# Last destination tile of the first attention: its high and low part in one set of weights, its chain on 160 columns

## The chip, the cores and the metric

The kernel runs on one core of one Trainium2 chip. The metric is the device time of one execution in microseconds. Before the change three runs gave 2427.32, 2428.82 and 2431.33 us; the median is 2428.82.

## The reference, cut to what matters

Four graph layers run one behind the other on 2708 nodes with 512 features. The change is in layer 0, whose attention is a softmax over the neighbours and a second softmax of the negated scores.

```python
def _L0_gnn_ref(inp, adj, W, a, wtrans):          # layer 0
    h = inp @ W
    e = leaky_relu(h @ a[:512] + (h @ a[512:]).T, 0.2)
    mask = adj > 0
    attention = softmax(where(mask, e, -1e12), axis=1)
    negative_attention = -softmax(where(mask, -e, -1e12), axis=1)
    h_prime_double = concatenate([attention @ inp, negative_attention @ inp], axis=1)
    return elu(h_prime_double @ wtrans)

def reference(x, adj, ...):                        # x: 2708 x 512, adj: 2708 x 2708
    h = maximum(layernorm(x), 0); x = x + _L0_gnn_ref(h, adj, ...)
    h = maximum(layernorm(x), 0); x = x + _L1_gnn_ref(h, adj, ...)   # 8 heads
    h = maximum(layernorm(x), 0); x = x + _L2_gnn_ref(h, adj, ...)   # weighted midpoint
    h = maximum(layernorm(x), 0); x = x + _L3_gnn_ref(h, adj, ...)   # dense scores
    return x
```

## The kernel before, in words

The 2708 nodes are padded to T = 22 tiles of 128. The last tile has 20 real rows (LAST = 20). The function `attention0` computes layer 0's attention with destinations in 11 blocks (IB = 11) of two tiles each, so that a block is 256 columns wide (BW). For each block `ib` and each source tile `j` there is a unit `m = 22 ib + j`; the last block is units 220 to 241, called units 0 to 21 of the last block below.

A unit goes through a chain over three engines. ScalarE makes the relu of the scores (`relu`), VectorE adds two rows for the two softmaxes (`scores`), ScalarE takes two exponentials (`exp`), VectorE multiplies with the mask (`mask`), ScalarE rounds to 16 bits (`high`, into `p_hi`), and VectorE takes what the rounding lost (`low`, into `p_lo`). `p_hi` and `p_lo` have five buffers (RP = 5); before it writes a buffer the chain waits for `p_used`, which TensorE counts up when it has done a unit. TensorE takes these as weights, 128 source rows by 128 destination columns, and multiplies with `z`, the features already multiplied with the layer's weights, also in a high and a low part. Each product has three terms: high by `z_hi`, high by `z_lo`, low by `z_hi`. Each term is a pair of matmuls with the same weights: 448 columns into `acc` and the other 64 (65 with the column of ones that gives the softmax's sum) into `side`. So `products` issues, for each of the two destination tiles (`q` is 0 or 1) and each of the two softmaxes (`s`), three pairs: 12 pairs a unit. The last source tile, `j` = 21, has only 20 rows, and there all terms are packed into one set of rows, so one matmul does for three.

TensorE's order is written out: in each block the first two units of tile 0, then the first two of tile 1, and after that both tiles of each unit. The engines run in order and wait for counters. When a block's sums are there, `denominator` makes the reciprocals on VectorE, `minus` and `minus_side` scale the negative half on ScalarE, `evacuate` and `evacuate_side` subtract on VectorE, `isolated` puts the mean in for nodes without neighbours, and `elu`, `plus` and `finish` add the result to x. For blocks 0 to 9 these steps are woven into the next block's chain. For block 10 they stand alone behind the last unit, and the next stage (`prep1`) starts after them.

SyncE's queue loads the mask and the rows of scores a block ahead, loads x, and stores x (`store_x`). Beside the chain the last block converts the mask to 8 bits (`convert`) and prepares the first rows for the next stage (`first_rows`, and a square root on ScalarE at `j` = 9).

Of the kernel before, what the change touches and what calls it, by code (L numbers as in the profile page):

```python
# [11 lines left out]
ALU = mybir.AluOpType  # L12
# [5 lines left out]
P = 128  # L18
# [583 lines left out]
def attention0(nc, dram, keep):  # L602
    with ExitStack() as stack:
# [17 lines left out]
        den = kit.sb("den", [2, 2])  # L621
        acc = kit.ps("acc", [3, 2, D])
# [13 lines left out]
            "blank_made v_packed z_packed ones_made os_made ys_made")  # L636

# [5 lines left out]
        with nc.Block() as block:  # L643
# [79 lines left out]
            def _(act):  # L723
                def relu(m):
# [7 lines left out]
                    act.activation(r[:, m % RR, :], u_row[:, ib % 2, :], ACT.Relu, bias=keep["v08"][:, j:j + 1],  # L732
                                   scale=0.8).then_inc(r_made, 1)

                def exp(m):
                    j = m % T
                    act.wait_ge(sc_made, m + 1)
                    if m >= RE:
                        act.wait_ge(pm_made, m - RE + 1)
                    act.activation(e[:, m % RE, 0], sc[:, m % RS, 0], ACT.Exp, bias=keep["v02"][:, j:j + 1])  # L740
                    act.activation(e[:, m % RE, 1], sc[:, m % RS, 1], ACT.Exp, bias=negv[:, j:j + 1], scale=-1.0).then_inc(e_made, 1)  # L741

                def high(m):
# [3 lines left out]
                    act.activation(p_hi[:, m % RP], pm[:, m % RM], ACT.Copy).then_inc(hi_made, 1)  # L747
# [24 lines left out]
                def minus(ib, q):  # L772
# [6 lines left out]
                    act.activation(o[:, q, 0:CA], acc[:, n % 3, 1, 0:CA], ACT.Identity, scale=den[:, q, 1:2], bias=one[:, 0:1]).then_inc(o_made, 1)  # L779

                def minus_side(ib):

                    for q in range(2):
                        act.activation(o[:, q, CA:D], side[:, ib % 2, q, 1, 0:DH], ACT.Identity, scale=den[:, q, 1:2], bias=one[:, 0:1]).then_inc(os_made, 1)
# [11 lines left out]
                for m in range(UNITS):  # L796
# [27 lines left out]
            def _(dve):  # L824
                def scores(m):
# [6 lines left out]
                    dve.tensor_tensor(sc[:, m % RS], r[:, m % RR, :].unsqueeze(1).broadcast_to([P, 2, BW]), g_row[:, ib % 2],  # L832
                                      ALU.add).then_inc(sc_made, 1)

                def mask(m):
# [8 lines left out]
                    dve.scalar_tensor_tensor(pm[:, m % RM], e[:, m % RE], TOP,  # L844
                                             at32[:, half, part, :].unsqueeze(1).broadcast_to([P, 2, BW]), ALU.min, ALU.mult).then_inc(pm_made, 1)

                def low(m):
# [2287 lines left out]
```

## Time and profile before

| | |
|---|---|
| median of three runs | 2428.82 us |
| the profiled execution: its own time | 2428.78 us |
| its span, from the first to the last instruction | 2426.9 us |
| TensorE busy | 2252.2 us, 93% of the span |
| VectorE busy | 1715.3 us, 71% |
| ScalarE busy | 1569.4 us, 65% |
| granted clock of TensorE, mean | 0.973 of full speed |
| matmuls of the first attention, first to last start | 176.2 to 807.5 us |

A row of the trace in order of time gives the start and the duration in microseconds, the engine (PE is TensorE, PEld its weight loads, DVE is VectorE, ACT ScalarE, SPq SyncE's queue), the line, what is written and read, the shape, and in brackets how long the engine had been idle and what ended that. For a matmul the shape is first rows*columns of the weights, then rows x columns of the moved operand. The recorded durations of matmuls overlap, since they are pipelined; what one costs in a row of many is the distance from start to start. Shares of the whole span are averages over stages; for a change in one stage the rows of that stage count.

### The profile page before, as it was taken

To read this page: it belongs to the slowest core of one execution; us is meant where nothing else is said; L and a number is where in the kernel's file an instruction comes from. 1 tells how busy PE (TensorE), PEld (TensorE's weight loads), DVE (VectorE), ACT (ScalarE), POOL (GpSimd) and SP (SyncE) were. 2 spreads that over 40 slices of the span, in tenths; PEclk is the share of its full clock that TensorE was granted. 3 is DMA by queue.
4 is the path that set the end of the run, shared out by engine and by line. 5 is a ranking of instruction groups with operands and counts; after the bars stand their busy time and mean duration, and the time that the engine had idled before them with its cause. 6 is when DMAs were issued, how large, how long until landed. Compare 5 with 4: busy or idle time off the path is not lost. (4 is left out here: it accounts for less than half of the span.)

```text
span 2426.9 us, 69291 instructions
## 1 busy us (share of the span) xinstructions
PE 2252.2 (93%) x29240; PEld 1469.5 (61%) x29240; DVE 1715.3 (71%) x3033; ACT 1569.4 (65%) x2622; POOL 35.3 (1%) x44
## 2 busy tenths in 40 slices
PE   7979999999999787999999867799989899999999
PEld 4535555555555447999999863355467545555554
DVE  5857888888887678999999965832467344556784
ACT  3448888888888468999999957521245444444452
POOL 1210000000000000000000000000000000000000
PEclk9989999999999898999999989999989999999999
DMA  4022222232222552121211125011111234334441
GB/s 176 9 80 66 84 84 84 85 100 95 84 83 86 185 191 64 34 52 52 51 52 52 60 64 177 13 37 41 32 70 49 79 102 125 106 103 130 114 129 36
DMA packets 224468, 201.05 MB, mean 83 GB/s; under 512 B 148972, under 2 KB 181906, under 8 KB 219964
## 3 DMA queue, kind: packets, MB, share of 16 engines
q1 hardware_dynamic: 222604, 189.11, 25.7%
q10 hardware_dynamic: 1584, 7.93, 1.0%
q8 instruction: 209, 3.42, 0.6%
q14 instruction: 71, 0.58, 0.1%
HBM read 145.37 MB, written 51.46 MB: 81 GB/s over the span
## 5 line engine op out<-in xcount | busy, mean ns | idle before, releaser
L1464 ACT ACTIVATE m_above<-keep_u,m_nvs 128x1408 fp8e5<-128x1408 f32 x318 | 435.5, 1453 | 0.0
L968 PE MATMUL m_acc<-keep_z_hi,m_p_hi 128*128 128x448 f16 x968 | 337.9, 353 | 19.8 <-DVE m_p_lo L852 16.9
L968 PE MATMUL m_acc<-keep_z_hi,m_p_lo 128*128 128x448 f16 x924 | 326.0, 353 | 0.0
L968 PE MATMUL m_acc<-keep_z_lo,m_p_hi 128*128 128x448 f16 x924 | 324.6, 351 | 0.0
L1805 PE MATMUL m_acc<-right_x_all,m_b 128*128 128x64 f16 x3872 | 242.6, 195 | 18.3 <-DVE m_b L1521 15.0
L1805 PE MATMUL m_acc<-right_x_all,m_c 128*128 128x64 f16 x3872 | 238.7, 194 | 14.4 <-DVE m_c L1529 11.2
L1805 PEld LDWEIGHTS m_acc<-right_x_all,m_b 128*128 128x128 fp8e5 x3872 | 233.7, 100 | 18.6 <-DVE m_b L1521 15.8
L1809 PE MATMUL m_acc<-right_x_all,m_b 128*128 128x64 f16 x3696 | 241.4, 195 | 1.8 <-issue 1.8
L1809 PE MATMUL m_acc<-right_x_all,m_c 128*128 128x64 f16 x3696 | 237.5, 194 | 4.0 <-issue 3.8
L1805 PEld LDWEIGHTS m_acc<-right_x_all,m_c 128*128 128x128 fp8e5 x3872 | 228.6, 99 | 16.5 <-DVE m_c L1529 12.9
L1809 PEld LDWEIGHTS m_acc<-right_x_all,m_b 128*128 128x128 fp8e5 x3696 | 230.0, 99 | 3.5 <-issue 3.3
L1809 PEld LDWEIGHTS m_acc<-right_x_all,m_c 128*128 128x128 fp8e5 x3696 | 226.4, 98 | 4.4 <-issue 4.4
L972 PE MATMUL m_side<-keep_z_hi,m_p_hi 128*128 128x65 f16 x968 | 183.6, 193 | 0.0
L972 PE MATMUL m_side<-keep_z_hi,m_p_lo 128*128 128x65 f16 x924 | 180.2, 195 | 0.0
L747 ACT ACTIVATE m_p_hi<-m_pm 128x512 f16<-128x512 f32 x242 | 151.3, 625 | 41.4 <-PE m_side L972 36.6
L844 DVE SCALAR_TENSOR_TENSOR m_pm<-m_e,m_at 128x512 f32<-128x512 f32 x242 | 166.6, 689 | 15.5 <-ACT m_e L741 3.7
L972 PE MATMUL m_side<-keep_z_lo,m_p_hi 128*128 128x64 f16 x924 | 177.2, 192 | 0.0
L2739 PE MATMUL m_acc<-keep_s_hi,m_wT_hi 128*128 128x512 f16 (+1 forms) x462 | 175.1, 379 | 0.0
L2741 PE MATMUL m_acc<-keep_s_hi,m_wT_lo 128*128 128x512 f16 (+1 forms) x462 | 175.1, 379 | 0.0
L2740 PE MATMUL m_acc<-keep_s_lo,m_wT_hi 128*128 128x512 f16 (+1 forms) x462 | 175.1, 379 | 0.0
L832 DVE TENSOR_TENSOR m_sc<-m_r,m_ug_row 128x512 f32<-128x512 f32 x242 | 166.1, 687 | 12.1 <-ACT m_r L732 10.6
L2968 ACT ACTIVATE m_lw<-m_sc 128x512 f32<-128x512 f32 (+3 forms) x70 | 32.1, 468 | 218.9 <-DVE m_mx L2785 188.8
(406 smaller groups left out, 5757.1 us busy)
## 6 DMA issues: line engine op xcount, KB each, us to landing
m_at<-adjT SPq DMA_DIRECT2D x11, 1408.0 KB, 7.0
m_at<-adjT SPq DMA_DIRECT2D x11, 1280.0 KB
keep_u<-rows SPq DMA_DIRECT2D x16, 704.0 KB, 4.1
low<-m_lw SPq DMA_DIRECT2D x32, 256.0 KB, 5.1
at<-edge_at SPq DMA_DIRECT2D x22, 352.0 KB, 3.2
keep_at<-at ACTq DMA_DIRECT2D x11, 704.0 KB, 6.5
keep_at_first<-at SPq DMA_DIRECT2D x22, 352.0 KB, 3.4
p_x_all<-x SPq DMA_DIRECT2D x4, 1536.0 KB, 10.3
```

The lines of the kernel that those rows point to most:

```text
L747: act.activation(p_hi[:, m % RP], pm[:, m % RM], ACT.Copy).then_inc(hi_made, 1)
L832: dve.tensor_tensor(sc[:, m % RS], r[:, m % RR, :].unsqueeze(1).broadcast_to([P, 2, BW]), g_row[:, ib % 2], ALU.add).then_inc(sc_made, 1)
L844: dve.scalar_tensor_tensor(pm[:, m % RM], e[:, m % RE], TOP, at32[:, half, part, :].unsqueeze(1).broadcast_to([P, 2, BW]), ALU.min, ALU.mu ...
L968: return pe.matmul(acc[:, n % 3, s, of], part(m, q, s, low), z[:, m % T, s, of], start=first, stop=last, skip_group_check=True)
L972: return pe.matmul(side[:, m // T % 2, q, s, 0:columns], part(m, q, s, low), z[:, m % T, s, CA:CA + columns], start=first, stop=last, skip ...
L1464: last = act.activation(above[:, q % RA, j - j0], u[:, g % RU], ACT.Relu, bias=nvs[:, g // NB, j:j + 1], scale=STEEP, saturate=False)
L1805: last = pe.matmul(to, mask, of[:, j0 + j, n, 0], start=(n == 0 and ch == 0 and j == 0 and t % 4 == 0), stop=(j0 + j == T - 1), skip_group ...
L1809: last = pe.matmul(to, mask, of[:, j0 + j, n, 1], start=False, stop=False, skip_group_check=True)
L2739: pe.matmul(acc[0:r, b, :], wT_hi[:, b, k, 0:r], s_hi[:, k, :], start=(k == 0), stop=False)
L2740: pe.matmul(acc[0:r, b, :], wT_hi[:, b, k, 0:r], s_lo[:, k, :], start=False, stop=False)
L2741: last = pe.matmul(acc[0:r, b, :], wT_lo[:, b, k, 0:r], s_hi[:, k, :], start=False, stop=False)
L2968: last = act.activation(lw[:, slot, 0:hi - lo], sc[:, q % SB, lo - n0:hi - n0], ACT.Copy)
```

## The change

In the last block the second destination tile has only 20 real columns. The change treats it as E = 32 columns. The chain of the last block works on 128 + 32 = 160 columns of each softmax in place of 256 (`width`). The low part of the 32 columns is written into `p_hi` directly behind the high part, so that one set of weights of 64 columns holds both. `products` calls `last_tile` for this tile: with `z_hi` it uses these 64 columns, and writes 64 rows of `acc` and `side` (high part in rows 0 to 31, low part in rows 32 to 63); with `z_lo` it uses the 32 columns of the high part. That makes two pairs for each softmax in place of three. Behind the last unit `move_low` copies rows 32 to 63 on ScalarE, and `add_low` and `add_wide` add them to rows 0 to 31 on VectorE. The flags of the rows from 32 on are filled with 1.0 by two memsets. `denominator` now waits for the first sum, and `minus` of the last tile for both.

```diff
+        E = 32
+        low_part, low_sum = kit.sb("low_part", [2, D]), kit.sb("low_sum", [2])
+        width = lambda m: BW if m < UNITS - T else P + E
+        rows_of = lambda ib, q: slice(0, E if (ib, q) == (IB - 1, 1) else P)
...
-                    act.activation(p_hi[:, m % RP], pm[:, m % RM], ACT.Copy).then_inc(hi_made, 1)
+                    act.activation(p_hi[:, m % RP, :, 0:width(m)], pm[:, m % RM, :, 0:width(m)], ACT.Copy).then_inc(hi_made, 1)
...
+                def move_low():
+
+                    act.wait_ge(acc_made, 2 * IB)
+                    act.activation(low_part[0:E, :, CA:D + 0], side[E:2 * E, (IB - 1) % 2, 1, :, 0:DH], ACT.Copy)
+                    act.activation(low_sum[0:E, :], side[E:2 * E, (IB - 1) % 2, 1, :, DH], ACT.Copy).then_inc(low_moved, 1)
+                    act.activation(low_part[0:E, :, 0:CA], acc[E:2 * E, (2 * IB - 1) % 3, :, 0:CA], ACT.Copy).then_inc(low_moved, 1)
...
+                move_low()
                 minus(IB - 1, 0)
                 minus_side(IB - 1)
                 minus(IB - 1, 1)
...
-                    if m % T < T - 1:
+                    if m % T == T - 1:
+                        low = p_hi[COPIES[2]:P, m % RP, :, 0:width(m)]
+                        dve.tensor_tensor(low, pm[COPIES[2]:P, m % RM, :, 0:width(m)], low, ALU.subtract).then_inc(lo_made, 1)
+                    elif m < UNITS - T:
                         dve.tensor_tensor(p_lo[:, m % RP], pm[:, m % RM], p_hi[:, m % RP], ALU.subtract).then_inc(lo_made, 1)
                     else:
-                        low = p_hi[COPIES[2]:P, m % RP]
-                        dve.tensor_tensor(low, pm[COPIES[2]:P, m % RM], low, ALU.subtract).then_inc(lo_made, 1)
+                        for to, of in ((p_lo[:, m % RP, :, 0:P], slice(0, P)), (p_hi[:, m % RP, :, P + E:P + 2 * E], slice(P, P + E))):
+                            last = dve.tensor_tensor(to, pm[:, m % RM, :, of], p_hi[:, m % RP, :, of], ALU.subtract)
+                        last.then_inc(lo_made, 1)
...
+                def add_low():
+                    dve.wait_ge(low_moved, 1)
+                    last = side[0:E, (IB - 1) % 2, 1]
+                    dve.tensor_tensor(last[:, :, 0:DH], last[:, :, 0:DH], low_part[0:E, :, CA:D], ALU.add)
+                    dve.tensor_tensor(last[:, :, DH], last[:, :, DH], low_sum[0:E, :], ALU.add).then_inc(low_added, 1)
+
+                def add_wide():
+                    dve.wait_ge(low_moved, 2)
+                    last = acc[0:E, (2 * IB - 1) % 3, :, 0:CA]
+                    dve.tensor_tensor(last, last, low_part[0:E, :, 0:CA], ALU.add).then_inc(low_added, 1)
...
+                add_low()
+                dve.wait_ge(low_added, 1)
                 denominator(IB - 1)
+                add_wide()
                 evacuate(IB - 1, 0)
+                dve.wait_ge(rden_made, IB)
+                for rows in (slice(E, 2 * E), slice(2 * E, P)):
+                    last = dve.memset(iso[rows, T - 1:T], 1.0)
+                last.then_inc(low_iso, 1)
+                dve.wait_ge(low_iso, 1)
                 evacuate_side(IB - 1)
                 evacuate(IB - 1, 1)
...
+                def last_tile(m, s, low, z, first):
+
+                    n, end = 2 * IB - 1, P + (2 * E if low else E)
+                    weights = p_hi[:, m % RP, s, P:end]
+                    to, columns = slice(0, end - P), DH + (z is z_hi)
+                    pe.matmul(acc[to, n % 3, s, 0:CA], weights, z[:, m % T, s, 0:CA], start=first, stop=False, skip_group_check=True)
+                    return pe.matmul(side[to, m // T % 2, 1, s, 0:columns], weights, z[:, m % T, s, CA:CA + columns],
+                                     start=False, stop=False, skip_group_check=True)
...
+                    if j < T - 1 and n == 2 * IB - 1:
+                        for s in range(2):
+                            for low, z in ((1, z_hi), (0, z_lo)):
+                                last = last_tile(m, s, low, z, j == 0 and z is z_hi)
+                        last.then_inc(p_used, 1)
+                        return
```

On TensorE, in a unit in the middle of the last block, the second destination tile stood in these rows before, for one of the two softmaxes (the name before the arrow is written, the first number is the number of weight columns, the second the columns moved):

```order
L968 MATMUL m_acc<-keep_z_hi,m_p_hi 128x448
L972 MATMUL m_side<-keep_z_hi,m_p_hi 128x65
L968 MATMUL m_acc<-keep_z_lo,m_p_hi 128x448
L972 MATMUL m_side<-keep_z_lo,m_p_hi 128x64
L968 MATMUL m_acc<-keep_z_hi,m_p_lo 128x448
L972 MATMUL m_side<-keep_z_hi,m_p_lo 128x65
```

With the change the same place, from the last matmul of the first tile to the second softmax of the last tile, reads:

```order
L1030 MATMUL m_side<-keep_z_hi,m_p_lo 128x65
L1015 MATMUL m_acc<-keep_z_hi,m_p_hi 64x448
L1016 MATMUL m_side<-keep_z_hi,m_p_hi 64x65
L1015 MATMUL m_acc<-keep_z_lo,m_p_hi 32x448
L1016 MATMUL m_side<-keep_z_lo,m_p_hi 32x64
L1015 MATMUL m_acc<-keep_z_hi,m_p_hi 64x448
```

Three pairs became two, and the number of weight columns goes from 128 to 64, to 32 and back to 64; behind the second softmax it goes from 32 back to 128.

On VectorE the end of the last block, from the last low part to the last add into x, was:

```order
L855 TENSOR_TENSOR m_p_hi<-m_pm,m_p_hi 64x512
L865 TENSOR_SCALAR keep_iso<-m_side 128x2
L867 SCALAR_TENSOR_TENSOR m_den<-keep_iso,m_side 128x4
L870 RECIPROCAL m_den<-m_den 128x4
L879 SCALAR_TENSOR_TENSOR m_y<-m_acc,m_den,m_o 128x448
L884 SCALAR_TENSOR_TENSOR m_y<-m_side,m_den,m_o 128x64 x2
L879 SCALAR_TENSOR_TENSOR m_y<-m_acc,m_den,m_o 128x448
L889 SCALAR_TENSOR_TENSOR m_y<-keep_cd,keep_iso,m_y 128x512 x2
```

With the change it is:

```order
L872 TENSOR_TENSOR m_p_hi<-m_pm,m_p_hi 64x2x160
L914 TENSOR_TENSOR m_side<-m_side,m_low_part 32x2x64
L915 TENSOR_TENSOR m_side<-m_side,m_low_sum 32x2
L888 TENSOR_SCALAR keep_iso<-m_side 128x2
L890 SCALAR_TENSOR_TENSOR m_den<-keep_iso,m_side 128x4
L893 RECIPROCAL m_den<-m_den 128x4
L920 TENSOR_TENSOR m_acc<-m_acc,m_low_part 32x2x448
L903 SCALAR_TENSOR_TENSOR m_y<-m_acc,m_den,m_o 128x448
L995 MEMSET keep_iso 32x1
L995 MEMSET keep_iso 64x1
L909 SCALAR_TENSOR_TENSOR m_y<-m_side,m_den,m_o 128x64
L909 SCALAR_TENSOR_TENSOR m_y<-m_side,m_den,m_o 32x64
```

Three adds and two memsets came in, two of the adds ahead of the reciprocal. On ScalarE the three copies of `move_low` stand ahead of `minus` in the same way.

## Rows read from the trace of the kernel before

**Rows 1.** Busy time by stretch: last block, then last attention's end; clock behind engines.

```profile
752.50:806.80 54.30, 54.23 (x492) 31.51 (x493) 42.00 (x72) 44.41 (x102) 0.00 (x0) 1.00 0.18 54
...
2408.65:2422.20 13.55, 13.55 (x69) 5.79 (x66) 0.83 (x4) 0.00 (x0) 0.00 (x0) 1.00 0.05 19
```

**Rows 2.** Waits of TensorE from 748 to 812: us, times, longest.

```profile
PE m_acc L968 <- PE m_acc L968: 0.3, 1, 0.3
PE m_acc L968 <- DVE m_p_lo L852: 0.3, 1, 0.3
```

**Rows 3.** TensorE in order of time, last block: start, duration.

```profile
750.79 0.35 PE L968 MATMUL m_acc<-keep_z_hi,m_p_hi 128*128 128x448 f16 x1 [0.30 <-PE m_acc L968]
...
752.57 0.36 PE L968 MATMUL m_acc<-keep_z_hi,m_p_hi 128*128 128x448 f16 x1 [0.29 <-DVE m_p_lo L852]
...
806.83 0.35 PE L968 MATMUL m_acc<-keep_z_hi,m_p_hi 128*128 128x448 f16 x1
...
807.34 0.54 PE L968 MATMUL m_acc<-keep_z_hi,m_p_hi 128*128 128x448 f16 x2
```

**Rows 4.** Order of time in the last attention: matmuls, then weight loads.

```profile
2321.77 0.38 PE L2737 MATMUL m_acc<-keep_s_hi,m_wT_hi 128*128 128x512 f16 x1
2321.98 0.38 PE L2680 MATMUL m_sc<-keep_e_hi 128*128 128x512 f16 x1
...
2391.32 0.38 PE L2737 MATMUL m_acc<-keep_s_hi,m_wT_hi 128*128 128x512 f16 x1
2391.63 0.18 PE L2680 MATMUL m_sc<-keep_e_hi 128*20 128x20 f16 x1
...
2391.91 0.17 PE L2680 MATMUL m_sc<-keep_e_hi,keep_e_lo 128*20 128x20 f16 x1
2392.01 0.28 PE L2695 MATMUL m_tw<-keep_ident,m_w_hi 128*128 128x128 f16 x2
...
2321.77 0.10 PEld L2680 LDWEIGHTS m_sc<-keep_e_hi 128*128 128x128 f16 x1
...
2391.62 0.09 PEld L2680 LDWEIGHTS m_sc<-keep_e_hi 128*20 128x20 f16 x1 [0.42 <-issue]
```

**Rows 5.** TensorE in order of time at the end of the last attention.

```profile
2408.65 0.38 PE L2739 MATMUL m_acc<-keep_s_hi,m_wT_hi 128*20 128x512 f16 x1
...
2422.24 0.38 PE L2737 MATMUL m_acc<-keep_s_hi,m_wT_hi 128*20 128x512 f16 x1
```

**Rows 6.** VectorE and ScalarE in order of time, last block.

```profile
750.63 0.68 DVE L832 TENSOR_TENSOR m_sc<-m_r,m_ug_row 128x512 f32<-128x512 f32 x1
751.22 0.69 DVE L844 SCALAR_TENSOR_TENSOR m_pm<-m_e,m_at 128x512 f32<-128x512 f32 x1
751.82 0.69 DVE L852 TENSOR_TENSOR m_p_lo<-m_pm,m_p_hi 128x512 f16<-128x512 f32 x1
...
750.75 0.73 ACT L779 ACTIVATE m_o<-m_acc,m_one,m_den 128x448 f32<-128x448 f32 x1 [5.41 <-DVE m_den L870]
...
790.72 0.63 ACT L747 ACTIVATE m_p_hi<-m_pm 128x512 f16<-128x512 f32 x1 [0.54 <-DVE m_pm L844]
```

**Rows 7.** Order of time at the end of the last block and behind it.

```profile
801.20 0.38 SPq L671 DMA_DIRECT2D m_x<-x  x1
...
807.59 0.16 DVE L865 TENSOR_SCALAR keep_iso<-m_side 128x2 f32<-128x2 f32 x1 [7.23 <-PE m_side L972]
...
808.19 0.72 ACT L779 ACTIVATE m_o<-m_acc,m_one,m_den 128x448 f32<-128x448 f32 x1 [8.55 <-DVE m_den L870]
808.82 0.69 ACT L784 ACTIVATE m_o<-m_side,m_one,m_den 128x64 f32<-128x64 f32 x2
809.13 0.68 DVE L879 SCALAR_TENSOR_TENSOR m_y<-m_acc,m_den,m_o 128x448 f32<-128x448 f32 x1 [0.97 <-ACT m_o L779]
...
812.44 1.23 DVE L894 SCALAR_TENSOR_TENSOR m_x<-m_y,m_x 128x1024 f32<-128x1024 f32 x1
...
814.95 0.36 SPq L675 DMA_DIRECT2D x<-m_x  x1
```

More of the change, by code:

```diff
@@ L731, in relu @@
                         act.wait_ge(sc_made, m - RR + 1)
-                    act.activation(r[:, m % RR, :], u_row[:, ib % 2, :], ACT.Relu, bias=keep["v08"][:, j:j + 1],
+                    act.activation(r[:, m % RR, 0:width(m)], u_row[:, ib % 2, 0:width(m)], ACT.Relu, bias=keep["v08"][:, j:j + 1],
                                    scale=0.8).then_inc(r_made, 1)
@@ L778, in minus @@
                         act.wait_ge(acc_made, n + 1)
[L779 removed]
+                    if n == 2 * IB - 1:
+                        act.wait_ge(low_added, 2)
+                    of = rows_of(ib, q)
+                    act.activation(o[of, q, 0:CA], acc[of, n % 3, 1, 0:CA], ACT.Identity, scale=den[of, q, 1:2], bias=one[of, 0:1]).then_inc(o_made, 1)
                 def minus_side(ib):
                     for q in range(2):
[L784 removed]
+                        of = rows_of(ib, q)
+                        act.activation(o[of, q, CA:D], side[of, ib % 2, q, 1, 0:DH], ACT.Identity, scale=den[of, q, 1:2], bias=one[of, 0:1]).then_inc(os_made, 1)
+                def move_low():
[3 more added lines that the diff above has]
+                    act.activation(low_part[0:E, :, 0:CA], acc[E:2 * E, (2 * IB - 1) % 3, :, 0:CA], ACT.Copy).then_inc(low_moved, 1)
                 def elu(ib):
@@ L831, in scores @@
                         dve.wait_ge(e_made, m - RS + 1)
-                    dve.tensor_tensor(sc[:, m % RS], r[:, m % RR, :].unsqueeze(1).broadcast_to([P, 2, BW]), g_row[:, ib % 2],
+                    w = width(m)
+                    dve.tensor_tensor(sc[:, m % RS, :, 0:w], r[:, m % RR, 0:w].unsqueeze(1).broadcast_to([P, 2, w]), g_row[:, ib % 2, :, 0:w],
                                       ALU.add).then_inc(sc_made, 1)
@@ L843, in mask @@
                         dve.wait_ge(lo_made, m - RM + 1)
-                    dve.scalar_tensor_tensor(pm[:, m % RM], e[:, m % RE], TOP,
-                                             at32[:, half, part, :].unsqueeze(1).broadcast_to([P, 2, BW]), ALU.min, ALU.mult).then_inc(pm_made, 1)
+                    w = width(m)
+                    dve.scalar_tensor_tensor(pm[:, m % RM, :, 0:w], e[:, m % RE, :, 0:w], TOP,
+                                             at32[:, half, part, 0:w].unsqueeze(1).broadcast_to([P, 2, w]), ALU.min, ALU.mult).then_inc(pm_made, 1)
                 def low(m):
@@ L964, in part @@
                     return (p_hi, p_lo)[low][:, m % RP, s, q * P:(q + 1) * P]
+                def last_tile(m, s, low, z, first):
[5 more added lines that the diff above has]
+                                     start=False, stop=False, skip_group_check=True)
                 def wide(m, n, q, s, low, z, first, last):
                     of = slice(0, CA)
+                    if n == 2 * IB - 1:
+                        return pe.matmul(acc[0:E, n % 3, s, of], p_hi[:, m % RP, s, P:P + E], z[:, m % T, s, of], start=first, stop=last, skip_group_check=True)
                     return pe.matmul(acc[:, n % 3, s, of], part(m, q, s, low), z[:, m % T, s, of], start=first, stop=last, skip_group_check=True)
@@ L971, in narrow @@
                     columns = DH + (z is z_hi)
+                    if m == UNITS - 1 and q == 1:
+                        return pe.matmul(side[0:E, m // T % 2, 1, s, 0:columns], p_hi[:, m % RP, s, P:P + E], z[:, m % T, s, CA:CA + columns],
+                                         start=first, stop=last, skip_group_check=True)
                     return pe.matmul(side[:, m // T % 2, q, s, 0:columns], part(m, q, s, low), z[:, m % T, s, CA:CA + columns],
```

11 lines of the change are left out of this document (7 added, 4 removed).

## The prediction

> **What bounds the kernel now.** I read the busy time by stretch first, then the waits of TensorE, then its instructions in order of time, then the same for the other engines in the last block and behind it. In the last block of the first attention TensorE is busy 54.23 of 54.30 us at the full clock (2.4 GHz), VectorE 42.00 and ScalarE 44.41 [rows 1]. In the whole block it is seen waiting twice, 0.3 us each time [rows 2]. So TensorE bounds this block. A pair of matmuls (448 columns, then 64 or 65) is the unit of cost: from 752.57 to 806.83 there are 246 such pairs (12 in each of 19 units, 18 left over from the first two), 54.26 us, that is 0.2206 us a pair with no stall in between [rows 3].
>
> Behind the block stands a chain in which nothing overlaps: sums, reciprocal, ScalarE's and VectorE's halves of the last tile, the final adds, the store at 814.95 [rows 7], and the next stage starts after it. What is added there is paid in full.
>
> **What the change removes.** In each of units 0 to 20 of the last block the last destination tile took six pairs and now takes four: 2 x 21 = 42 pairs, 42 x 0.2206 = 9.3 us. The moved columns stay 448 and 64 or 65, and the trace shows that weights of few columns do not make a matmul shorter: in the last attention, with 20-column weights, the 512-column matmuls start every 0.216 us (63 steps from 2408.65 to 2422.24), as with 128 columns [rows 4, 5]. So the gain is pairs alone. Nor does the clock fall with narrow weights: 1.00 granted in that stretch [rows 1].
>
> **The stall at the block's start.** VectorE there does scores, mask and low part one behind the other, 0.68 or 0.69 us each, from 750.63 to 752.51 [rows 6], and TensorE, whose six pairs from 750.79 end at about 752.11, starts the next at 752.57 [rows 3]. With 320 elements in place of 512, each of the first two shrinks by about 0.2 us (0.69 for 512, 1.23 for 1024 [rows 6, 7], so 0.54 per 512), the split third by some 0.1. Low parts are then there near 752.05: the stall of 0.46 goes, I take 0.4. Bounds: 0 and 0.5.
>
> **What the change adds on TensorE.** Here is the term that decides. The order of instructions shows that the weights change their number of columns all the time: 128, 64, 32, 64, 32, 128. That is five changes in each unit; units 0 and 1 lie together and have nine. With 19 units of five and three changes in unit 21, that is 9 + 95 + 3 = 107 changes. Before there are none in this block. The trace has few such changes, but it has them. In the last attention the step from a 512-column matmul with 128-column weights to the next with the same kind is 0.21 (2321.77 to 2321.98). Where the next has 20-column weights the step is 0.31 (2391.32 to 2391.63), and on the way back, after a 20-column matmul of which its like start 0.025 apart (eleven steps from 2391.63 to 2391.91), it is 0.10 [rows 4]. The rows of weight loads show the same: normally a load starts with the matmul before it, 2321.77; here it starts at 2391.62, only 0.01 before its own matmul, after 0.42 us of idle time marked "issue" [rows 4]. So both steps are the streaming time plus about 0.095 us: 512 columns take 0.213, 20 take 0.008. All changes of the new order come behind a 64- or 65-column matmul, which streams 0.027 and whose usual step is 0.03; the step becomes 0.12, so I take 0.09 for each: 107 x 0.09 = 9.6 us. The rows show 128 to 20 columns and back; for 64 to 32 and back, which they don't show, I take the same, since a change of the column count is what the delayed rows have in common. Bounds of the price: 0 (if these rows wait for something else), and 0.26 if weight load (0.10) and matmul (0.19) stood end to end in place of 0.03.
>
> The Trainium skill, "TensorEngine Tiling (Array Packing)", Key Properties, says that changing the tiling mode, not just the tile, drains TensorE, and it lists 128 x 64 and 128 x 32 as modes of their own; by that rule all five changes of a unit count, and the rows just read agree for 128 to 20 columns and back. For 64 to 32 no row here shows it. The same page, under Restrictions, says that column tiling switches fast weight load off, which speaks against the change as well: behind a change of mode the slower load of 64 columns would stand open. No row here has weights of 64 columns, and the sum holds nothing for it.
>
> If only changes from and to 128 cost something, 43 count (19 units with two, two in the joint group of units 0 and 1, three in unit 21): 3.9 us. That is a rival below.
>
> **What it adds behind the block.** Before: TensorE's last pair ends at 807.88 (807.34 and 0.54 [rows 3]), but VectorE starts at 807.59, since only the first tile's products are waited for; ScalarE starts at 808.19 [rows 7]. Now ScalarE must wait for all products (0.35 later), copies the low part's 2 x 64 side sums (0.44: 0.39 for 64 elements, since two take 0.69 with about 0.09 of overlap, and 0.72 for 448 [rows 7], so 0.33 per 384), then the two sums (0.2), and only then may VectorE add them (0.3 for 128 elements and 0.16 for two, like its short operations at 807.59 [rows 7]), with a step between engines of about 0.05 each: the reciprocal moves back by about 1.4. ScalarE copies the wide part (2 x 448, 1.10 by the same slope) meanwhile. VectorE's add of it (896 elements, 1.1 by 1.23 for 1024) comes before its part of the first tile; before, it idled 0.97 there [rows 7], so +0.1. Two fills of the isolated flags and a wait for them: +0.3. The copies of 32 partitions in place of 128 save nothing, since the time goes by elements per partition. Sum 1.8 us; bounds 1.0 (copies and adds overlap better) and 2.8 (each signal costs 0.15 more).
>
> **What else could be late.** Narrower relu, exp, mask and copies only give ScalarE and VectorE more room while TensorE's unit stays at 10 x 0.2206 + 5 x 0.09 = 2.66 us against 2.65 before. The mask, the u rows and x are loaded by the same queue in the same order; TensorE's speed does not move a wait of it. x for the final add is issued at 801.20 before and needed at 812.44 [rows 7]; that stays.
>
> **Sum** against the profiled execution: -9.3 - 0.4 + 9.6 + 1.8 = +1.7 us. Its span is 2426.9, its own time 2428.78, so 2430.5; the median of the three runs, 2428.82, gives the same 2430.5. A difference of under 0.2% (4.9 us) is what a measurement of this kernel cannot tell from none.
>
> **Rivals.**
> 1. Changes of width cost nothing: the 0.31 and 0.10 are waits for data. For it: two events are few. Against it: the 0.42 us are marked as issue, not as a release by an engine, and the same line opens its chunk at 2321.98 with no delay. Then TensorE needs 2.21 us a unit, and ScalarE, which is never idle from 750.75 until just before 790.72 [rows 6] while TensorE takes 2.65, comes near its own limit in the middle of the block: I put 0.4 us of new stalls. -9.3 - 0.4 + 0.4 + 1.8 = -7.5: 2421.3. Chance 0.10.
> 2. Only changes from or to 128 columns cost: -9.3 - 0.4 + 3.9 + 1.8 = -4.0: 2424.8. For it: all that the rows show is of this kind. Chance 0.13.
> 3. Slower: each change costs more, because the weights of 64 columns are loaded in the open behind the drain. Place: TensorE between the 32- or 128-column matmul and the 64-column one, 42 of the 107 changes. The point from which it decides is (4.9 + 9.3 + 0.4 - 1.8) / 107 = 0.12 us a change; at 0.13 the sum is +6.0: 2434.8. For it: the rows know only 20-column weights, which are the shortest to load. Against it: the way back loads 128 columns in the open, and still costs 0.10 in all [rows 4]. Chance 0.15.
>
> **Chances.** The forecast has 0.62; its own range is 2428 to 2433.5 (0.075 to 0.095 a change, 1.0 to 2.8 behind the block). Slower by over 0.2%: 0.15 from rival 3 and 0.04 from the forecast's edge, 0.19. Faster: rival 1 (0.10) and 0.03 of rival 2, 0.13. Within 0.2%: 0.68. The range for 8 in 10 runs from 2423.5 (all of rival 2) to 2434.8, and leaves out rival 1 and half of rival 3.
>
> **What would show it.** Right: in the last block the first matmul behind each change of width starts about 0.12 us after the 64- or 65-column one before it, its weight load begins with it and not before it, and from the first pair to the last the block takes about as long as before, 56 us, though it has 42 pairs less. The store of the last x comes 1.8 us later behind TensorE's last matmul than before. The stall near 752 is gone. Wrong: steps of 0.03 at the changes (then it is faster by 7 us or so), steps of 0.03 only between 64 and 32, steps over 0.15, or TensorE waiting for VectorE's low parts in the middle of the block.

## The result, and the profile after

The changed kernel takes 2434.19 us, the median of 20 runs (2428.62 to 2442.61). The kernel before, run beside it, takes 2430.98 us, also of 20 runs (2427.32 to 2437.22). The ratio is 1.0018, with a 95% interval of 1.0010 to 1.0025: the changed kernel is slower by 4.4 us, at least 2.4 and at most 6.1. (The two medians alone differ by 3.2 us, which lies inside that interval.) That is just under the 0.2% that I had named as the border of what can be told from no change, yet the interval leaves no change out. The forecast for the profiled execution was 2430.5 against 2428.78, a loss of 1.7 us. It started from three runs of the kernel before, whose median is 2.2 us below that of its twenty runs here; so of the way from 2430.5 to 2434.19 a part belongs to the starting point and not to the change.

| us | before | after |
|---|---|---|
| span of the profiled execution | 2426.9 | 2433.4 |
| its own time | 2428.78 | 2435.21 |
| first pair of the last block starts | 750.79 | 753.34 |
| last two wide matmuls start | 807.34 | 811.79 |
| store of the last x is issued | 814.95 | 820.65 |
| **block**: first pair to last wide matmuls | 56.55 | 58.45 |
| **tail**: from there to the store | 7.61 | 8.86 |

The block is 1.90 us longer and the tail 1.25: 3.15 us in the two parts that the change touches. The other 3.35 us by which the two spans differ lie ahead of the first pair (2.55) and behind the store (0.8), where nothing was changed. A difference of that kind comes without any change too: when the kernel before is run again (e5), its span is 2.1 us longer, with block and tail the same. Whether the change has a part in it is taken up under what stays open. So from here on block and tail are the measure, and the whole times stand beside them.

How the block came to be longer, TensorE's rows tell. First the view by stretch, for the same stretch as before [rows 1]: stretch, its length, then busy time and number of records of TensorE, weight loads, VectorE, ScalarE and GpSimd, then the clock.

```profile
752.50:806.80 54.30, 54.00 (x397) 24.60 (x395) 34.71 (x97) 38.86 (x105) 0.00 (x0) 1.00 0.20 54
```

TensorE is still busy in 54.00 of 54.30 us, where it was 54.23. But it has started 397 matmuls in that time, and before 492. The busy share hides the loss: a matmul's record is longer (0.19 us for 65 columns) than the distance at which matmuls follow (0.03), so the records overlap, and a gap of 0.1 us between two starts leaves no idle time. VectorE and ScalarE have lost 7.3 and 5.6 us of work, as their narrower operations should bring.

Next one unit of the changed kernel in order of time (start, duration, engine, line, operation, written<-read, shape of the weights, shape moved), with the start of the next unit's last tile at the end:

```profile
776.65 0.38 PE L1015 MATMUL m_acc<-keep_z_hi,m_p_hi 128*64 128x448 f16 x1
776.86 0.19 PE L1016 MATMUL m_side<-keep_z_hi,m_p_hi 128*64 128x65 f16 x1
776.99 0.36 PE L1015 MATMUL m_acc<-keep_z_lo,m_p_hi 128*32 128x448 f16 x1
777.18 0.19 PE L1016 MATMUL m_side<-keep_z_lo,m_p_hi 128*32 128x64 f16 x1
...
777.64 0.36 PE L1015 MATMUL m_acc<-keep_z_lo,m_p_hi 128*32 128x448 f16 x1
777.84 0.19 PE L1016 MATMUL m_side<-keep_z_lo,m_p_hi 128*32 128x64 f16 x1
777.97 0.36 PE L1023 MATMUL m_acc<-keep_z_hi,m_p_hi 128*128 128x448 f16 x1
778.17 0.20 PE L1030 MATMUL m_side<-keep_z_hi,m_p_hi 128*128 128x65 f16 x1
778.20 0.35 PE L1023 MATMUL m_acc<-keep_z_lo,m_p_hi 128*128 128x448 f16 x1
...
779.40 0.38 PE L1015 MATMUL m_acc<-keep_z_hi,m_p_hi 128*64 128x448 f16 x1
```

A unit takes 2.75 us (776.65 to 779.40), and before 2.65. Inside one width a step from a narrow matmul to the next wide one is 0.03 (778.17 to 778.20). At each change of width it is 0.12 or 0.13 (776.86 to 776.99, 777.84 to 777.97). The rows are rounded to 0.01; the mean over all 107 changes of the block is 0.1245, against 0.0306 inside one width. The matmul behind a change also takes a little longer to the next start: for the wide ones the mean is 0.213 us with 64 columns of weights, 0.200 with 32 and 0.200 with 128, in place of 0.190.

The weight loads of the same stretch (idle time ahead of them in brackets) show what else is different there:

```profile
776.98 0.09 PEld L1015 LDWEIGHTS m_acc<-keep_z_lo,m_p_hi 128*32 128x32 f16 x1 [0.20 <-issue]
...
777.97 0.10 PEld L1023 LDWEIGHTS m_acc<-keep_z_hi,m_p_hi 128*128 128x128 f16 x1 [0.21 <-issue]
...
778.17 0.10 PEld L1023 LDWEIGHTS m_acc<-keep_z_lo,m_p_hi 128*128 128x128 f16 x1
```

Within a width a load runs beside the matmul ahead of its own: that of 778.20 starts at 778.17. Behind a change it starts only with its own matmul (776.98 for 776.99), after 0.20 us in which nothing is loaded. It is what [rows 4] had shown once, at 2391.62. What goes on inside TensorE in that time, no row shows.

The waits of the weight loads from 745 to 830 count these places (waited for: us, times, longest):

```profile
PEld m_acc L1015 <- issue: 15.6, 76, 0.2
...
PEld m_acc L1023 <- issue: 4.5, 19, 0.7
PEld m_acc L1015 <- DVE m_p_hi L877: 1.5, 7, 0.2
...
PEld m_side L1028 <- issue: 0.4, 2, 0.2
PEld m_acc L1023 <- DVE m_p_hi L877: 0.4, 2, 0.2
...
PEld m_acc L1015 <- DVE m_p_hi L872: 0.2, 1, 0.2
```

Together 107 waits. One, the longest, is that of the block's first load (0.7), which the kernel before has too. The other 106 are of 0.2 us and stand at changes of width. Ten of the 106 are put down to VectorE, whose operation merely ended last; they last as long as the others. The 107th change, from 811.29 to 811.43 in the last unit, shows as a step of 0.14 without a wait.

At the block's start VectorE and TensorE read as follows (of before: [rows 3, 6]):

```profile
753.57 0.48 DVE L863 SCALAR_TENSOR_TENSOR m_pm<-m_e,m_at 128x320 f32<-128x320 f32 x1
753.98 0.42 DVE L877 TENSOR_TENSOR m_p_lo<-m_pm,m_p_hi 128x256 f16<-128x256 f32 x1
754.31 0.22 DVE L877 TENSOR_TENSOR m_p_hi<-m_pm,m_p_hi 128x64 f16<-128x64 f32 x1
```

```profile
753.34 0.35 PE L1023 MATMUL m_acc<-keep_z_hi,m_p_hi 128*128 128x448 f16 x1 [0.30 <-PE m_acc L1023]
...
754.63 0.20 PE L1030 MATMUL m_side<-keep_z_hi,m_p_lo 128*128 128x65 f16 x1
754.66 0.35 PE L1023 MATMUL m_acc<-keep_z_hi,m_p_hi 128*128 128x448 f16 x1
```

The operation with the mask takes 0.48 us in place of 0.69, the two for the low part together 0.55 in place of 0.69. The low parts are ready by 754.53, before TensorE wants them at 754.66. The stall that ended at 752.57 before [rows 3] is gone.

Behind the block, ScalarE and VectorE in order of time:

```profile
812.37 0.27 ACT L798 ACTIVATE m_low_part<-m_side 32x128 f32<-32x128 f32 x1 [11.77 <-PE m_acc L1022]
812.55 0.15 ACT L799 ACTIVATE m_low_sum<-m_side 32x2 f32<-32x2 f32 x1
812.60 0.90 ACT L800 ACTIVATE m_low_part<-m_acc 32x896 f32<-32x896 f32 x1
813.79 0.72 ACT L787 ACTIVATE m_o<-m_acc,m_one,m_den 128x448 f32<-128x448 f32 x1 [0.29 <-DVE m_den L893]
```

```profile
812.80 0.29 DVE L914 TENSOR_TENSOR m_side<-m_side,m_low_part 32x128 f32<-32x128 f32 x1 [11.67 <-ACT m_low_sum L799]
813.01 0.15 DVE L915 TENSOR_TENSOR m_side<-m_side,m_low_sum 32x2 f32<-32x2 f32 x1
813.19 0.16 DVE L888 TENSOR_SCALAR keep_iso<-m_side 128x2 f32<-128x2 f32 x1
...
813.67 1.06 DVE L920 TENSOR_TENSOR m_acc<-m_acc,m_low_part 32x896 f32<-32x896 f32 x1
814.72 0.68 DVE L903 SCALAR_TENSOR_TENSOR m_y<-m_acc,m_den,m_o 128x448 f32<-128x448 f32 x1
```

The chain is the one that the prediction described, with smaller steps: VectorE's sums start 1.40 us behind the last wide matmuls (813.19 less 811.79), before 0.25 [rows 7]. That is 1.15 of the 1.25 us by which the tail is longer; the rest stands behind `evacuate`, where the two fills are.

### The profile page after: what moved, and what is told of

Read it like the earlier page. It is cut to its first block and busy times, and to the rows that moved or that the text cites. A ratio compares the mean times of both kernels' runs of the same rounds, so it can differ in the third digit from the quotient of the medians.

```text
span 2433.4 us, 69155 instructions
## 1 busy us (share of the span) xinstructions
PE 2258.6 (93%) x29156; PEld 1463.7 (60%) x29156; DVE 1705.7 (70%) x3059; ACT 1562.1 (64%) x2625; POOL 35.4 (1%) x44
## 5 line engine op out<-in xcount | busy, mean ns | idle before, releaser
L1023 PE MATMUL m_acc<-keep_z_hi,m_p_hi 128*128 128x448 f16 x924 | 323.3, 354 | 21.0 <-DVE m_p_lo L874 18.1
L1023 PE MATMUL m_acc<-keep_z_hi,m_p_lo 128*128 128x448 f16 x882 | 311.4, 353 | 0.0
L1023 PE MATMUL m_acc<-keep_z_lo,m_p_hi 128*128 128x448 f16 x882 | 310.3, 352 | 0.0
L752 ACT ACTIVATE m_p_hi<-m_pm 128x512 f16<-128x512 f32 (+1 forms) x242 | 148.0, 612 | 48.1 <-PE m_side L1030 38.6
L1030 PE MATMUL m_side<-keep_z_hi,m_p_hi 128*128 128x65 f16 x924 | 175.7, 194 | 0.0
L863 DVE SCALAR_TENSOR_TENSOR m_pm<-m_e,m_at 128x512 f32<-128x512 f32 (+1 forms) x242 | 162.3, 671 | 15.7 <-ACT m_e L746 4.0
L850 DVE TENSOR_TENSOR m_sc<-m_r,m_ug_row 128x512 f32<-128x512 f32 (+1 forms) x242 | 161.7, 669 | 15.0 <-ACT m_r L737 13.5
L1030 PE MATMUL m_side<-keep_z_hi,m_p_lo 128*128 128x65 f16 x882 | 172.1, 195 | 0.0
L1030 PE MATMUL m_side<-keep_z_lo,m_p_hi 128*128 128x64 f16 x882 | 169.4, 192 | 0.0
```

The lines of the kernel that those rows point to most:

```text
L752: act.activation(p_hi[:, m % RP, :, 0:width(m)], pm[:, m % RM, :, 0:width(m)], ACT.Copy).then_inc(hi_made, 1)
L850: dve.tensor_tensor(sc[:, m % RS, :, 0:w], r[:, m % RR, 0:w].unsqueeze(1).broadcast_to([P, 2, w]), g_row[:, ib % 2, :, 0:w], ALU.add).then ...
L863: dve.scalar_tensor_tensor(pm[:, m % RM, :, 0:w], e[:, m % RE, :, 0:w], TOP, at32[:, half, part, 0:w].unsqueeze(1).broadcast_to([P, 2, w]) ...
L1023: return pe.matmul(acc[:, n % 3, s, of], part(m, q, s, low), z[:, m % T, s, of], start=first, stop=last, skip_group_check=True)
L1030: return pe.matmul(side[:, m // T % 2, q, s, 0:columns], part(m, q, s, low), z[:, m % T, s, CA:CA + columns], start=first, stop=last, skip ...
```

## The experiments

Nine more runs were made: six kernels with an edit, and three repeats (e5, e7, e8). "Local" is block and tail together, from each kernel's own profiled execution; before it is 64.16, after 67.31. The ratios are of whole times.

| | block | tail | local against before | ratio, 95% interval |
|---|---|---|---|---|
| after | 58.45 | 8.86 | +3.15 | 1.0018, 1.0010 to 1.0025 |
| e1 one width | 46.71 | 8.85 | -8.60 | 0.9975, 0.9966 to 0.9984 |
| e2 three changes | 53.85 | 8.86 | -1.45 | 1.0004, 0.9993 to 1.0015 |
| e3 64 only | 51.62 | 8.86 | -3.68 | 1.0001, 0.9991 to 1.0010 |
| e4 end only | 56.54 | 8.86 | +1.24 | 1.0006, 0.9997 to 1.0016 |
| e5 before again | 56.54 | 7.61 | -0.01 | 0.9998, 0.9989 to 1.0008 |
| e6 chain only | 56.07 | 7.72 | -0.37 | 0.9999, 0.9989 to 1.0009 |
| e7 after again | 58.44 | 8.86 | +3.14 | 1.0019, 1.0009 to 1.0028 |
| e8 one width again | 46.72 | 8.85 | -8.59 | 0.9974, 0.9964 to 0.9984 |
| e9 narrow first | 58.45 | 8.86 | +3.15 | 1.0021, 1.0011 to 1.0030 |

My theory was that each change of the weights' width costs TensorE a fixed time, whichever two widths it lies between, and that the pairs themselves cost what they did. The rivals were those of the prediction: changes are free and something else waits, only changes from and to 128 cost, or the loads of 64 columns cost more than the others.

**e1, one width.** Undoes the changes of width. The last tile takes four pairs a unit as in the changed kernel, but always with 128 columns of weights, and all its 128 rows are written. The columns behind the real ones hold what the buffer held; their rows are not read.

```diff
-        width = lambda m: BW if m < UNITS - T else P + E
+        width = lambda m: BW if m < UNITS - T or m == UNITS - 1 else P + E
-                    weights = p_hi[:, m % RP, s, P:end]
-                    to, columns = slice(0, end - P), DH + (z is z_hi)
+                    weights = p_hi[:, m % RP, s, P:2 * P]
+                    to, columns = slice(0, P), DH + (z is z_hi)
...
-                    if n == 2 * IB - 1:
-                        return pe.matmul(acc[0:E, n % 3, s, of], p_hi[:, m % RP, s, P:P + E], z[:, m % T, s, of], start=first, stop=last, skip_group_check=True)
...
```

> The two pairs for each softmax of the last tile stay, but their weights are always 128 columns wide (high part, low part, then 64 columns whose results nobody reads), and the last unit works at full width, so that no matmul of the block changes the width of its weights. Theory A, each change of width costs about 0.11 us: all 107 changes go, TensorE takes 2.21 us a unit; from the first pair of the last block to its last wide matmuls 47 to 47.5 us (56.5 before, 58.4 with the change), to the store of the last x 56 us (64.2 before); time 0.34% under before, some 2420.5 to 2422 beside 2429. Theory B, the change is slow for what it adds behind the block and for its narrow chain, and the widths matter little: the block takes 56 us or more and the time stays at or above before.

The block takes 46.71 us, 11.74 less than in the changed kernel. The whole, 2424.29 us in the median, came out 0.25% under before and not the 0.34% expected; the 2.5 us between the two lie outside block and tail (see what stays open). Its rows, in order of time, at the place shown above for the changed kernel:

```profile
776.99 0.20 PE L1025 MATMUL m_side<-keep_z_hi,m_p_lo 128*128 128x65 f16 x1
777.03 0.35 PE L1015 MATMUL m_acc<-keep_z_hi,m_p_hi 128*128 128x448 f16 x1
777.22 0.19 PE L1016 MATMUL m_side<-keep_z_hi,m_p_hi 128*128 128x65 f16 x1
777.25 0.35 PE L1015 MATMUL m_acc<-keep_z_lo,m_p_hi 128*128 128x448 f16 x1
```

No step from a narrow matmul to the next is longer than 0.04, and the only wait of a weight load in the block is that of its first. Against the kernel before the block is 9.84 shorter, where 42 pairs at 0.2206 and the stall of 0.46 make 9.73. So the pairs were worth what was forecast, and inside the block the changes of width are all that had eaten them. This version is faster than both kernels.

**e2, three changes in a unit.** The same pairs with the loops in `last_tile`'s caller exchanged: both softmaxes with 64 columns, then both with 32. Of the 107 changes 42 go, all between 64 and 32.

```diff
-                        for s in range(2):
-                            for low, z in ((1, z_hi), (0, z_lo)):
+                        for low, z in ((1, z_hi), (0, z_lo)):
+                            for s in range(2):
```

> The changed kernel, but the last tile's pairs are put in another order: 64-column weights of both softmaxes first, then 32-column weights of both. 65 changes of width are left of 107, nothing else differs. Theory A (0.11 us for each change, whichever widths): block 58.4 - 42 x 0.109 = 53.9 us, first pair to store 62.7 us, 1.4 under before and 4.6 under the changed kernel. Rival C, only changes from and to 128 columns cost: block as in the changed kernel, 58.4.

The block is 4.60 us shorter than the changed kernel's: 0.1095 for each of the 42. TensorE in order of time, in the last tile of one unit:

```profile
777.05 0.20 PE L1016 MATMUL m_side<-keep_z_hi,m_p_hi 128*64 128x65 f16 x1
777.08 0.35 PE L1015 MATMUL m_acc<-keep_z_hi,m_p_hi 128*64 128x448 f16 x1
777.27 0.19 PE L1016 MATMUL m_side<-keep_z_hi,m_p_hi 128*64 128x65 f16 x1
777.40 0.36 PE L1015 MATMUL m_acc<-keep_z_lo,m_p_hi 128*32 128x448 f16 x1
777.60 0.19 PE L1016 MATMUL m_side<-keep_z_lo,m_p_hi 128*32 128x64 f16 x1
777.62 0.35 PE L1015 MATMUL m_acc<-keep_z_lo,m_p_hi 128*32 128x448 f16 x1
```

From 64 to 64 and from 32 to 32 the step is 0.03 and 0.02, from 64 to 32 it is 0.13. Two 64-column weights of different softmaxes follow each other without delay, so it is the width that counts and not that other weights are read. Rival 2, by which only changes from and to 128 cost, is refuted.

**e3, 64 columns only.** All four pairs of the last tile use the 64 columns; the product of both low parts, which was left out before, is added as well. Then 43 changes are left, all from or to 128 columns.

```diff
-                            for low, z in ((1, z_hi), (0, z_lo)):
+                            for low, z in ((1, z_hi), (1, z_lo)):
```

> The changed kernel, but the product with the low part of z uses the 64 columns too (its low rows get one small term more). 43 changes of width are left, all between 128 and 64 but for three at the end. Theory A: block 58.4 - 64 x 0.109 = 51.5 us, first pair to store 60.3 us, 3.8 under before. Rival D, what costs is the load of 64-column weights and not the change: block at 58 or more, since there are twice as many such loads.

The block is 6.83 us shorter than the changed kernel's: 0.107 for each of 64 changes. Against e1 it is 4.91 longer: 0.114 for each of the 43 left. Inside the tile the pairs follow at the full rate:

```profile
778.58 0.38 PE L1015 MATMUL m_acc<-keep_z_hi,m_p_hi 128*64 128x448 f16 x1
778.80 0.19 PE L1016 MATMUL m_side<-keep_z_hi,m_p_hi 128*64 128x65 f16 x1
778.83 0.35 PE L1015 MATMUL m_acc<-keep_z_lo,m_p_hi 128*64 128x448 f16 x1
779.02 0.19 PE L1016 MATMUL m_side<-keep_z_lo,m_p_hi 128*64 128x64 f16 x1
779.05 0.35 PE L1015 MATMUL m_acc<-keep_z_hi,m_p_hi 128*64 128x448 f16 x1
```

Only the first step behind the change is longer (0.22 from 778.58, then 0.19 from 778.83). A pair is 0.22 us, as with 128 columns. So weights of 64 columns are not slow to load in a row; the rule of the Trainium skill that I had held against the change ("TensorEngine Tiling (Array Packing)", Restrictions: column tiling switches fast weight load off) shows here as no more than that 0.02 or 0.03 us. The page's other rule (Key Properties: a change of mode drains TensorE) agrees with e1, e2 and e3: there is a price at each change, for 64 to 32 columns as well, which no row of the kernel before had shown. The runs show the delay; that it is a drain they do not show.

**e4, end only.** The kernel before with the copies, adds and fills behind the block and nothing else. It adds rows 32 to 63 of the last accumulator, which here hold nothing of the low part.

```diff
+                move_low()
                 minus(IB - 1, 0)
...
+                add_low()
+                dve.wait_ge(low_added, 1)
...
+                add_wide()
...
+                for rows in (slice(E, 2 * E), slice(2 * E, P)):
+                    last = dve.memset(iso[rows, T - 1:T], 1.0)
...
```

> The kernel before with what the change adds behind the block, and nothing else: the three copies, the three adds (here of zeros, since the destinations from 20 on have no edges), the two memsets and their waits. Theory A: block as before, 56.5 us; from the last wide matmuls to the store 8.9 us in place of 7.6, time 1.3 us above before (0.05%, within the noise). Theory B: 4 us above before.

The tail is 8.86 us, to the hundredth that of the changed kernel, and the block that of the kernel before. So the tail's cost is 1.25 us, and it is the same with the old block ahead of it. The ratio fits (+1.5 us, -0.7 to +3.9).

**e5, before again,** is the kernel before without an edit, and **e7, after again,** the changed kernel without one, both in one comparison.

> The kernel before, unchanged, once more: what a ratio and a trace vary by themselves. Both theories: ratio 1.000 +- 0.001; block 56.5 us, first pair to store 64.2. If its first matmul of the first attention starts near 176.2 again while all changed ones start at 177.3 to 178.9, something that every changed kernel shares delays the start; if it lies among them, the start differs by chance.

> The changed kernel, unchanged, beside the kernel before once more. Theory A: block 58.4, first pair to store 67.3, that is 3.15 us or 0.13% more than before; the ratio should come out at 1.0013, and the measured 1.0018 (1.001 to 1.0025) holds it.

Block and tail came out within 0.01 us of the first profiles. The spans are 2429.0 and 2432.6, in place of 2426.9 and 2433.4: the difference between two spans moves by 2.9 us with nothing changed. The unchanged kernel compares at 0.9998, the changed at 1.0019, which is +4.6 us (2.2 to 6.8): the loss is there again. The question about the start was not settled. The first matmul of the first attention starts at 176.9 in e5, between the two values named; it starts at 176.0 in e6 and at 177.2 to 178.9 in all eight profiles that have the added copies, 1.3 us later in the mean than in the three without them. One profile of each kernel does not tell whether the added instructions have to do with it.

**e6, chain only.** The narrow chain of 160 columns, with three pairs of 128 columns for the last tile as before, and behind the block only the two fills. The low part is kept in a buffer of its own.

```diff
-                    dve.tensor_tensor(p_lo[:, m % RP], pm[:, m % RM], p_hi[:, m % RP], ALU.subtract).then_inc(lo_made, 1)
+                    w = width(m)
+                    dve.tensor_tensor(p_lo[:, m % RP, :, 0:w], pm[:, m % RM, :, 0:w], p_hi[:, m % RP, :, 0:w], ALU.subtract).then_inc(lo_made, 1)
...
-                    if j < T - 1 and n == 2 * IB - 1:
...
```

> The changed kernel's chain of 160 columns and its two memsets alone: the products are as before, three pairs for each softmax with 128-column weights (the columns beyond the 32 give rows that nobody reads), no copies and adds behind the block, last unit at full width. Theory A: only the stall of 0.46 us at the start of the block goes, block 56.1; end 7.9 (7.6 and the memsets); first pair to store 64.0. Theory B (the narrow chain is what costs): block over 57.

The block is 56.07, 0.48 less than before: the stall at its start and nothing more. The narrower chain is worth just that stall, since TensorE bounds the block [rows 1]. The tail is 0.11 longer; the two fills of the flags stand in it.

**e8, one width again,** is e1 once more, since a version that beats both kernels should be seen twice.

> The kernel of one width again, unchanged. From the first pair of the block to the store of the last x it was 8.6 us under before (55.56 against 64.16), but the ratio of whole times was 0.9975 (0.9966 to 0.9984), that is 6.1 us. If the rest of the gain is given back behind the block, the ratio stays near 0.9975 and the stretch behind the store is longer than before's 1612 by 2 us or more; if it was chance, the ratio lies nearer to 0.9965.

Local -8.59 us, ratio 0.9974 (0.9964 to 0.9984): the gain is there again, and so is the gap between local and whole. Behind the store e8 takes 1614.0 us, 2.0 more than before; but e5 and before, the same kernel, already differ by 0.7 there.

**e9, narrow first.** The changed kernel with the matmul on 64 or 65 columns issued ahead of the one on 448 in each pair of the last tile. Then most changes of width stand behind a long matmul, and if the price were a weight load that only lacks cover, it would be hidden.

```diff
-                    pe.matmul(acc[to, n % 3, s, 0:CA], weights, z[:, m % T, s, 0:CA], start=first, stop=False, skip_group_check=True)
-                    return pe.matmul(side[to, m // T % 2, 1, s, 0:columns], weights, z[:, m % T, s, CA:CA + columns],
-                                     start=False, stop=False, skip_group_check=True)
+                    pe.matmul(side[to, m // T % 2, 1, s, 0:columns], weights, z[:, m % T, s, CA:CA + columns],
+                              start=False, stop=False, skip_group_check=True)
+                    return pe.matmul(acc[to, n % 3, s, 0:CA], weights, z[:, m % T, s, 0:CA], start=first, stop=False, skip_group_check=True)
```

> The changed kernel with the two matmuls of each pair of the last tile in the other order, 64 or 65 columns first and 448 behind, so that 84 of the 107 changes of width come behind a 448-column matmul. Theory A, a change costs a fixed time on top of the streaming of the one before it: block as in the changed kernel, 58.4 us. Rival E, the cost is what a short matmul cannot cover (a weight load that a long one would hide): most of 84 x 0.109 = 9 us goes, block near 50.

Block 58.45, as without the edit. TensorE in order of time, in the last tile:

```profile
778.53 0.22 PE L1015 MATMUL m_side<-keep_z_hi,m_p_hi 128*64 128x65 f16 x1
778.58 0.36 PE L1017 MATMUL m_acc<-keep_z_hi,m_p_hi 128*64 128x448 f16 x1
778.87 0.20 PE L1015 MATMUL m_side<-keep_z_lo,m_p_hi 128*32 128x64 f16 x1
778.90 0.35 PE L1017 MATMUL m_acc<-keep_z_lo,m_p_hi 128*32 128x448 f16 x1
```

Behind the wide matmul the step at a change is 0.29 (778.58 to 778.87), where it is 0.19 without a change: 0.10 us more, as behind a narrow one. And the 0.02 of the first step now lies on the narrow matmul (778.53 to 778.58). Rival E, which put the block near 50, is refuted: the price isn't hidden behind a long matmul.

## Why the prediction came out wrong

Its sum was -9.3 - 0.4 + 9.6 + 1.8 = +1.7 us. Term by term:

- **Pairs removed, -9.3: right.** e1 has the 42 pairs less and none of the changes, and its block is 9.84 shorter, 9.73 with the stall expected.
- **Stall at the block's start, -0.4: right.** e6 isolates it: -0.48.
- **Changes of width, 107 at 0.09 = +9.6: the mechanism and the count right, the size wrong.** 58.45 less 56.55, with the 9.26 and 0.46 added that were gained, is 11.62 us, or 0.109 a change; e1, which has none of the changes, gives 11.74 directly. e2 and e3 give 0.1095 and 0.107 by taking changes away, and the 43 that e3 keeps cost 0.114 each. I had priced only the step from the last matmul in the old width to the first in the new, and that was nearly right: it is 0.094 longer than usual in the mean, 10.05 us in all. The next step, from the first matmul in the new width to its partner, I had put at nothing. It is 0.01 longer with 32 or 128 columns and 0.02 with 64, and comes to 1.6 us in all. So of the 2.0 us by which the term was too small, 0.4 lie in the rounding of the price and 1.6 in the step that was left out. The trace of the kernel before would have shown that step: behind its change at 2391.63 the next start comes after 0.03 in place of 0.025. It was not looked at.
- **The tail, +1.8: right in kind, too large.** It is 1.25 (after, e4, e7 and e9 alike). The reciprocal moved back by 1.15 and not 1.4: I took ScalarE's copy of 128 elements as 0.44 and that of 896 as 1.10 from rows on 128 partitions; they take 0.27 and 0.90, and two sums take 0.15, not 0.2. The fills cost 0.11 (e6) in place of 0.3, and the wide add nothing in place of 0.1. That this term was 0.55 too large hid a quarter of the other error; that was luck.
- **Other engines: right.** In the block TensorE waits for no other engine.

With the measured sizes the sum is -9.26 - 0.46 + 11.62 + 1.25 = +3.15 us. (It closes by itself, since 11.62 was taken as the remainder; the independent check is e1's 11.74.) On the forecast's starting point that is 2431.9, within its own range of 2428 to 2433.5; the measured median, 2434.19, lies above that range, and inside the wider one for 8 in 10 runs only. What failed is the call that this could not be told from no change. The step of the text that failed is "so I take 0.09 for each": each change costs 0.109. Rival 3 set the point from which it becomes slower at 0.12 a change, and with the tail at 1.25 in place of 1.8 that point would have been 0.125. So by the local sum the change stays below 0.2%, as the ratio's middle does (0.18%); but twenty runs on each side tell differences of 0.1%, and I had set that limit too coarsely.

Rival 1 (changes are free) and rival 2 (only those from and to 128 columns) are refuted, by the changed kernel's rows and by e2. Rival 3's mechanism, a dearer load of 64 columns in the open, is worth 0.01 us more for the matmul that follows than a change to another width (0.213 against 0.200), not the 0.04 it would have needed.

**What stays open.** The whole times are less favourable than block and tail. For e4 to e6, which keep all the pairs, they agree within 0.5 us. For the kernels with fewer pairs they don't: +4.4 against +3.15 for the changed kernel is within the interval, but for e3 +0.2 us (-2.2 to +2.4) stands against -3.68, and for e1 -6.1 (-8.3 to -3.9) against -8.60. So some 1 to 4 us seem to be lost outside the block. The stretch behind the store can't show it in one profile each: it is 1611.95 and 1612.6 for the unchanged kernel, 1613.3 and 1614.0 for e1 and e8, 1612.75 and 1612.96 for the changed kernel, but 1610.4 for e2, 1608.05 for e4 and 1615.5 for e9. A part of the scatter goes with TensorE's granted clock, which falls to 0.50 (1.2 GHz) now and then outside the block, as from 170 to 175 us of the kernel before, where TensorE was idle. Outside block and tail e4 takes 2360.9 us at a mean clock of 0.974, before, e2 and e6 take 2362.7 to 2363.2 at 0.973, and e5 and after 2364.9 and 2366.1 at 0.971. But e3 takes 2365.6 at 0.973, and at 0.972 e7 takes 2365.3, e1 and e8 2367.0 and 2367.1, and e9 2368.0: e1, e3, e8 and e9 take more than that order gives them. What in it depends on the block was not found; that a part of a gain is given back later is only likely.

Nor is "a change of width costs 0.11" shown for every matmul. In the last attention of the kernel before, a matmul in f32 with 20-column weights stands between others of 128 columns:

```profile
2393.17 0.16 PE L2709 MATMUL m_misc<-keep_ones,m_wT_lo 128*128 128x1 f16 x1
2393.20 0.27 PE L2716 MATMUL m_misc<-keep_ident,m_mm 128*20 128x128 f32 x1
2393.30 0.38 PE L2739 MATMUL m_acc<-keep_s_hi,m_wT_hi 128*128 128x512 f16 x1
```

Its step is 0.03 ahead and 0.11 behind, as without a change (0.11 is what most of its like with 128 columns take), and the one with 66 columns at 162.03 starts 0.22 us behind a 512-column matmul, with no delay either. On the other hand the step is 0.31 in place of 0.215 where the number of weight rows falls from 128 to 20 with 128 columns kept (2396.32 to 2396.63, in f32, and 2407.17 to 2407.48, in f16). So the price found here holds for matmuls in f16; no run asks what decides it in general.

## What to carry to other kernels

Count how often the order of f16 matmuls changes the number of weight columns, and price each change at about 0.11 us before saving pairs of 0.22 by narrower weights: here 107 changes ate 42 pairs. Keep the weights of one width (fill the tile up with whatever columns are there) or put all matmuls of a width together. Where a price is multiplied by a hundred, read it over two steps, from the start before the event to the second start behind it. Then let the spread of that product, and not the sum's middle, set the chances.

## What was not expected of the hardware

- A change of width costs the same 0.11 us between 64 and 32 columns (0.1095) as between 128 and narrower (0.114), and 0.09 to 0.10 of it falls between the last matmul in the old width and the first in the new, whether that last one streams 65 columns or 448 (e9).
- Rows of f16 matmuls with 64 or 32 columns of weights, all of one width, run at the rate of 128 columns: a pair is 0.22 us in e2 and e3. Narrow weights save nothing and cost nothing by themselves.
- ScalarE's plain copy on 32 partitions took 0.27 us for 128 elements and 0.90 for 896. The copy with scale and bias took 0.72 for 448 on 128 partitions and 0.70 on 32 (the changed kernel's last tile, 814.99). So it is not the partitions that make it shorter; by the slope of the two plain copies (0.63 per 768) 448 elements would take 0.53 us, an estimate. What the scale and the bias add was not tried on its own.
